# Graph layer on one core: the node table in groups of four blocks, loads and stores reordered

## What is computed

```python
h = relu(layernorm(x))                        # per node
l0 = h[:, :64] @ W_l1_0 * a / sqrt(64)        # node table, a = node_vec1
l1 = einsum('nud,uw->nwd', h[:, 64:], W_l1_1) * a / sqrt(32)
w  = relu(edge_attr_10 @ W_fc1 ...) @ W_fc2   # 192 weights per edge
y0, y1 = l0[src], l1[src]                     # gather per edge
m  = products of w, y0, y1 and edge_attr_4    # messages
s  = segment_sum(m, dst)                      # per node
out = x + self-interaction(h) + s @ W_l2
```

## Time and profile before

| | us |
|---|---|
| median of 3 runs | 4271.78 (4270.87 to 4272.3) |
| the profiled execution | 4272.76 |
| its span in the profile | 4268.9 |
| PE busy (share of the span) | 3722.5 (87%) |
| POOL busy | 3100.0 (73%) |
| DVE busy | 2009.8 (47%) |
| ACT busy | 1025.5 (24%) |
| mean granted clock of PE | 0.791 |

### The profile page before, as it was taken

The page is one execution under the profiler, slowest core; times in us unless marked ns, Lnnn a source line. Parts: engine busy times, 40 slices in busy tenths (PEclk is TensorE's granted clock), DMA queues, the critical chain, the costliest instruction groups (busy, mean ns, idle before and its releaser), DMA issues.

```text
span 4268.9 us, 57575 instructions
## 1 busy us (share of the span) xinstructions
PE 3722.5 (87%) x17362; PEld 2092.9 (49%) x17362; DVE 2009.8 (47%) x6987; ACT 1025.5 (24%) x2226; POOL 3100.0 (73%) x3265
## 2 busy tenths in 40 slices
PE   7988888888888888889888888888888888888887
PEld 6644444444444444444444544554444454444444
DVE  5345444444544444444444444444444444444443
ACT  3322222222222222222222222222222222222222
POOL 1277777777777777777777777777777777777775
PEclk9978777787777878777877877777788787877877
DMA  5245455555555454555545455554545555455454
GB/s 173 68 125 140 130 136 131 137 132 132 136 134 138 129 137 131 135 131 137 139 130 138 128 138 135 133 138 129 137 131 137 137 131 138 130 136 139 129 138 109
DMA packets 717859, 566.78 MB, mean 133 GB/s; under 512 B 394563, under 2 KB 646098, under 8 KB 717168
## 3 DMA queue, kind: packets, MB, share of 16 engines
q0 software_dynamic: 155008, 265.22, 26.1%
q1 hardware_dynamic: 562064, 297.63, 24.4%
q10 hardware_dynamic: 480, 0.19, 0.0%
HBM read 414.55 MB, written 148.11 MB: 132 GB/s over the span
## 4 chain that ended last, share of the span: by engine, by line
POOL 35%; DMA 25%; PE 17%; issue 14%; DVE 9%; SPq 0%; ACT 0%; ACTq 0%; DVEq 0%; POOLq 0%
POOL R L588 35%; DMA R<-l_table,src 24%; DVE R L696 6%; PE bank L734 5%; PE bank L461 3%; DVE R L693 3%; PE bank L724 2%; PE bank L747 2%; PE bank L304 1%; PE bank L302 1%; PE bank L291 1%; PE bank L503 0%; PE bank L292 0%; DMA av<-in_avec 0%; PE bank L484 0%
## 5 line engine op out<-in xcount | busy, mean ns | idle before, releaser
L588 POOL DMA_INDIRECT R<-l_table,src x3223 | 3070.1, 953 | 1003.3 <-issue 799.6
L734 PE MATMUL bank<-w,hs 100*128 100x192 f32 x6446 | 1685.4, 404 | 510.0 <-DVE R L696 504.0
L734 PEld LDWEIGHTS bank<-w,hs 100*128 100x128 f32 x6446 | 1302.7, 233 | 1124.2 <-issue 1062.0
L693 DVE TENSOR_TENSOR R<-bank,R 128x256 f32<-128x256 f32 x1612 | 682.1, 423 | 2057.1 <-DMA R<-l_table,src 1115.5
L696 DVE TENSOR_TENSOR R<-bank,R 128x192 f32<-128x192 f32 x3224 | 984.6, 347 | 0.0
L654 ACT ACTIVATE E<-bank 128x320 f32<-128x320 f32 x806 | 352.3, 437 | 2390.2 <-PE bank L747 2345.1
L747 PE MATMUL bank<-R 128*32 128x320 f32 x6448 | 758.7, 550 | 0.0
L724 PE MATMUL bank<-ea,w1s 10*100 10x512 f32 x1612 | 569.5, 789 | 0.8 <-ACT hs L648 0.8
L648 ACT ACTIVATE hs<-bank 100x512 f32<-100x512 f32 x806 | 436.7, 594 | 391.3 <-PE bank L724 390.7
L461 PE MATMUL bank<-Z,D 128*128 128x448 f32 x784 | 419.5, 690 | 6.3 <-DMA Z<-s_tiles 6.3
L461 PEld LDWEIGHTS bank<-Z,D 128*128 128x128 f32 x784 | 184.1, 248 | 267.6 <-issue 260.0
(11 more groups left out here) (69 smaller groups left out, 771.7 us busy)
## 6 DMA issues: line engine op xcount, KB each, us to landing
s_tiles<-E SPq DMA_DIRECT2D x806, 160.0 KB
R<-l_table,src POOLq DMA_INDIRECT x3223
ea<-in_ea_p SPq DMA_DIRECT2D x403, 96.0 KB
Z<-s_tiles SPq DMA_DIRECT2D x392, 96.0 KB
Z<-s_tiles SPq DMA_DIRECT2D x392, 80.0 KB
Z<-s_tiles SPq DMA_DIRECT2D x392, 48.0 KB
x<-in_xp SPq DMA_DIRECT2D x14, 560.0 KB, 7.1
l_table<-ls SPq DMA_DIRECT2D x14, 560.0 KB, 3.1
```

Source lines behind the costliest of these rows:

```text
L588: PL.indirect_dma_start(out=Y[:, g % NB, t, :], out_offset=None, in_=T, in_offset=bass.IndirectOffsetOnAxis(ap=src[:, k:k + 1], axis=0),). ...
L693: V.tensor_tensor(p[:, :, :, 0:64], w[:, :, 0:128].rearrange("p t (s c) -> p t s c", s=2), y[:, :, 0:64].unsqueeze(2).to_broadcast([128, n ...
L734: m = PE.matmul(b[:, o * 192:(o + 1) * 192], hs[:, g % 4, t * 128:(t + 1) * 128], w2[:, :], start=True, stop=True, skip_group_check=True)
```

## The change

It regroups the table stage by four blocks, 640 columns, which are five times 128:

- `centre` writes into one buffer `H` (2 x 640 columns), whichever engine it is on.
- `turn(q)` transposes five full 128x128 parts of four blocks; a part can hold the end of one block and the beginning of the next.
- `lin(q)` multiplies by five pieces of a block-diagonal 640x640 matrix, laid out on the host as `bl` (128x704): three of 128 columns, two of 160 that overlap in 32 columns, where the two halves of a block are added in PSUM.
- `keep_wide` (DVE, 512 columns at once) and `keep_fifth` (ACT) copy the transposed parts; `row_out` reads five pieces for four blocks (block 2 lies in two banks).
- `ls` holds 3 x 4 blocks, and SP stores every four, 25 stores instead of 14.
- SP's queue has all of x first; the scaling of the weights on DVE moves behind the first statistics; ACT runs one square root ahead of everything; the end of the window test and the flag move to the end of the stage.

Core of the diff:

```diff
-        hn = sb("hn", [128, 3, C])
-        hp = sb("hp", [128, 2, C])
-        hta = sb("hta", [128, 2, 256])
-        htb = sb("htb", [32, 2, 256])
-        ls = sb("ls", [128, 2, LC, C])
+        H = sb("H", [128, 2, 4 * C])
+        hta = sb("hta", [128, 2, 512])
+        htb = sb("htb", [128, 2, 128])
+        ls = sb("ls", [128, 3, 4, C])
...
         for c in range(NLC):
             SP.dma_start(x[:, c * LC:(c + 1) * LC, :], xv[:, c * LC:(c + 1) * LC, :]).then_inc(s_x[c], 16)
-            if c == 1:
-                SP.dma_start(bas[:, :, :], a["bases"].rearrange("o (g t) -> o g t", t=G).to_broadcast([128, NG, G])
-                             ).then_inc(s_b, 16)
...
+        SP.dma_start(bound[:, :, :], a["bound"]).then_inc(s_b, 16)
...
         def row_out(j):
-            c, jj = divmod(j, LC)
+            q, b = divmod(j, 4)
             if j % BC == 0:
                 AC.wait_ge(s_ar, j // BC + 1)
...
+            if b == 0 and q >= 3:
+                AC.wait_ge(s_T[q % 3], 16 * (q // 3))
+            fore, rear = bank[4 + q % 2], bank[6 + q % 2]
...
+        def turn(q):
+
+            if q >= 2:
+                PE.wait_ge(s_ha, q - 1)
+                PE.wait_ge(s_hb, q - 1)
+            for j in blocks(q):
+                if j % 3 == 2:
+                    PE.wait_ge(s_hp, third.index(j) + 1)
+                else:
+                    PE.wait_ge(s_hn, others.index(j) + 1)
+                b = j % 4
+                m = PE.transpose(bank[q % 2][:, b * 128:(b + 1) * 128], H[:, q % 2, b * 128:(b + 1) * 128], ident[:, :])
...
+            PE.transpose(bank[2 + q % 2][:, 0:128], H[:, q % 2, 512:640], ident[:, :]).then_inc(s_tp, 1)
+
+        def lin(q):
+            fore, rear = bank[4 + q % 2], bank[6 + q % 2]
+            PE.wait_ge(s_ha, q + 1)
+            if q >= 2:
+                PE.wait_ge(s_lv, rows_out(q - 2))
+            for b in range(3):
+                k = slice(b * 128, b * 128 + 128)
+                m = PE.matmul(fore[:, k], hta[:, q % 2, k], bl[:, k], start=True, stop=True, skip_group_check=True)
+            m.then_inc(s_lp, 1)
+            PE.matmul(rear[:, 0:160], hta[:, q % 2, 384:512], bl[:, 384:544], start=True, stop=False,
                       skip_group_check=True)
+            PE.wait_ge(s_hb, q + 1)
+            PE.matmul(rear[:, 96:256], htb[:, q % 2, :], bl[:, 544:704], start=False, stop=True,
                       skip_group_check=True).then_inc(s_lp, 1)
...
+        for q in range(NQ + 2):
+            if q >= 2:
+                for j in blocks(q - 2):
+                    row_out(j)
+            if 1 <= q <= NQ:
+                keep_fifth(q - 1)
+            if q + 1 < NQ:
+                for j in blocks(q + 1):
+                    centre(j)
+            if q in batch:
+                root(batch[q])
...
         stats(0)
+        map_weights()
         stats(1)
         deviations(0)
-        nst, ndv = 2, 1
+        nst = 2
         pieces = test()
-        for i in range(NT // 2):
+        for q in range(NQ):
+            while nst < NLC and nst * LC < 4 * q + 16:
                 stats(nst)
                 nst += 1
+            keep_wide(q)
+            if q in batch:
+                deviations(batch[q])
+            if q == min(10, NQ - 1):
                 main_weights()
+            if q >= 8:
                 next(pieces, None)
...
-        for c in range(NLC):
-            SP.wait_ge(s_lv, (c + 1) * LC)
-            SP.dma_start(tv[:, c * LC:(c + 1) * LC, :], ls[:, c % 2, :, :]).then_inc(s_T[c % 2], 16)
+        for q in range(NQ):
+            n = len(blocks(q))
+            SP.wait_ge(s_lv, rows_out(q))
+            SP.dma_start(tv[:, 4 * q:4 * q + n, :], ls[:, q % 3, 0:n, :]).then_inc(s_T[q % 3], 16)
```

More of the change, by code:

```diff
@@ L151, in build @@
         s_ha = sem("s_ha")
-        s_hb = [sem("s_hb0"), sem("s_hb1")]
+        s_hb = sem("s_hb")
         s_lp = sem("s_lp")
         s_lv = sem("s_lv")
-        s_T = [sem("s_T0"), sem("s_T1")]
+        s_T = [sem(f"s_T{b}") for b in range(3)]
         s_one = sem("s_one")
@@ L295, in lin @@
[L295 to L302, removed]
+            if b == 0 and q >= 3:
+                AC.wait_ge(s_T[q % 3], 16 * (q // 3))
+            fore, rear = bank[4 + q % 2], bank[6 + q % 2]
+            if b == 0:
+                AC.wait_ge(s_lp, 2 * q + 1)
@@ L303, in lin @@
                       skip_group_check=True)
-            PE.matmul(ov[:, 128:160], htb[:, i % 2, o * 128:o * 128 + 128], blb[:, :], start=False, stop=True,
+            PE.wait_ge(s_hb, q + 1)
+            PE.matmul(rear[:, 96:256], htb[:, q % 2, :], bl[:, 544:704], start=False, stop=True,
                       skip_group_check=True).then_inc(s_lp, 1)
-        FP = max(NT // 2 - 7, 1)
         PE.wait_ge(s_w, NW)
-        PE.wait_ge(s_pw, 1)
-        for j in range(NT + 3):
-            if j < NT:
-                turn(j)
-            if j >= 3:
-                lin(j - 3)
-            if j == 2 * FP + 4:
+        for q in range(NQ + 1):
+            if q < NQ:
+                turn(q)
+            else:
@@ L317, in build @@
                 PE.wait_ge(s_fl, 1)
                 PE.wait_ge(s_one, 1)
-                PE.matmul(bank[2][32:33, 0:1], vio[:, 8:9], ones[:, :], start=True, stop=True,
+                PE.matmul(bank[q % 2][0:1, 0:1], vio[:, 8:9], ones[:, :], start=True, stop=True,
                           skip_group_check=True).then_inc(s_fl, 1)
-        LAG = 6
-        AC.wait_ge(s_w, NW)
-        root(0)
-        for j in range(NT + LAG):
-            if j < NT and j % BC == BC - 3 and j + 3 < NT:
-                root(j // BC + 1)
-            if j < NT:
-                centre(j)
-            if j >= 3 and j % 2 and (j - 3) // 2 < NT // 2:
-                narrow((j - 3) // 2)
-            if j >= LAG:
-                row_out(j - LAG)
-            if j == 2 * FP + 5:
+            if q == 1:
+                PE.wait_ge(s_pw, 1)
@@ new lines, in build @@
+            if q:
+                lin(q - 1)
+        batch = {-(-c * BC // 4): c for c in range(1, NBC)}
+        AC.wait_ge(s_one, 1)
+        AC.activation(warm[:, :], ones[:, :], ACT.Sqrt)
+        for j in blocks(0):
+            centre(j)
+        root(0)
+        for q in range(NQ + 2):
+            if q >= 2:
+                for j in blocks(q - 2):
[4 more added lines that the diff above has]
+                for j in blocks(q + 1):
+                    centre(j)
+            if q in batch:
+                root(batch[q])
+            if q == NQ:
@@ L335, in build @@
                 AC.wait_ge(s_fl, 2)
-                AC.activation(flag[0:1, 0:1], bank[2][32:33, 0:1], ACT.Copy).then_inc(s_fs, 1)
+                AC.activation(flag[0:1, 0:1], bank[q % 2][0:1, 0:1], ACT.Copy).then_inc(s_fs, 1)
         def test():
@@ L549, in table_there @@
         def table_there():
-            PL.wait_ge(s_T[0], 16 * ((NLC + 1) // 2))
-            PL.wait_ge(s_T[1], 16 * (NLC // 2))
+            for b in range(3):
+                PL.wait_ge(s_T[b], 16 * ((NQ + 2 - b) // 3))
         with nc.If(way == 0):
@@ L916, in lay_out @@
     ea_p[:, 32:42] = both[:, 1]
-    bla = np.zeros((128, 128), f)
-    bla[0:64, 0:64] = v["L0_gnn_W_l1_0"]
-    bla[64:96, 64:96] = v["L0_gnn_W_l1_1"]
-    bla[96:128, 96:128] = v["L0_gnn_W_l1_1"]
+    one = np.zeros((C, C), f)
+    one[0:64, 0:64] = v["L0_gnn_W_l1_0"]
+    for d in range(3):
+        one[64 + 32 * d:96 + 32 * d, 64 + 32 * d:96 + 32 * d] = v["L0_gnn_W_l1_1"]
+    four = np.zeros((4 * C, 4 * C), f)
+    for b in range(4):
+        four[b * C:(b + 1) * C, b * C:(b + 1) * C] = one
+    bl = np.concatenate([four[128 * b:128 * b + 128, o:e] for b, (o, e) in
+                         enumerate(((0, 128), (128, 256), (256, 384), (384, 544), (480, 640)))], axis=1)
     pw = np.zeros((5 * 128, C), f)
```

101 lines of the change are left out of this document (52 added, 49 removed).

## The result

| | kernel before | changed kernel |
|---|---|---|
| median of 4 runs (us) | 4271.61 (4270.87 to 4272.3) | 4196.35 (4193.85 to 4196.62) |
| span of the profiled execution (us) | 4268.9 | 4192.6 |
| first gather starts (us) | 185.3 | 108.3 |
| last gather starts (us) | 4236.6 | 4161.8 |

The changed kernel is faster by 75.3 us, a ratio of 0.9823 (95% interval 0.9806 to 0.984). The forecast was 4204.5 with a range of 4190 to 4214. The first gather was forecast at 118.0 and came 9.7 earlier.

The account below looks back on a forecast made before the run. POOL's gathers bound the kernel, PE the table stage before them. 43.0 + 5.2 + 62.1 + 2.5 + 1.1 + 0.2 = 114.1 put the first gather at 118.0, saving 67.3 us: 4204.5, range 4190 to 4214.

Parts of the forecast that it names:

- rival 1: Table stage: PE's clock rises, DVE and ACT pace at 2.9 to 3.0 us per four, 4194.5 us; chance 0.24.
- What bounds: Main stage: POOL's gathers pace it; only what the table stage saves before the first gather comes off the whole.
- PE's four at 1.2 GHz: Table stage: PE takes 3.45 us per four blocks, bounds 3.4 and 4.15, as nearly nothing changes shape.
- The stall: Table stage: ACT stops some 15 us until the first table store, queued behind the loads, lands at 43.0 (38 to 45).
- Rival 2: First table store not held behind the loads: no stall, first gather near 106, 4192.5 us; chance 0.08.
- I keep 1.2 GHz: Table stage: PE's clock stays at 1.2 GHz under the new instruction mix, as in the old stage.
- the charge for DVE: Table stage: 1.1 us (0 to 6) where main-weight scaling falls beside a window-test piece and statistics.
- Level with PE: Table stage: DVE's work per four sums to 3.5 us, about PE's 3.45.
- The other engines: Table stage, per four: ACT 2.4 us and POOL 1.1, both hidden below PE's 3.45.
- Rival 3: Table stage: PE still pays for shapes, or DVE paces; 3.85 us per four, 4212.5 us; chance 0.13.
- rival 4: Main stage passes from POOL to PE at mean clock 0.65: slower, 4394 us; chance 0.02.
- The start gains: Start of table stage: early x and the root's table load ahead of time are worth nothing, hidden by the stall.

Follow-up runs that it names:

- all three cures: Changed kernel with six-four row buffer, later stages' loads behind table stores, main-weight scaling on POOL instead of DVE: 4156.28 us against 4273.37 for the kernel before.
- kernel with 128 rows: Kernel before with second transpose 128 columns wide and second product over 128 rows, 96 against zeros: ratio 0.9866, repeated 0.9871.
- x first: Kernel before with only SP's loads reordered, all of x first in the queue, run twice: ratios 0.9998 and 1.0003.
- wide transpose: Kernel before with second transpose 128 columns wide, second product on rows 96 to 127 alone: 5260.32 us against 5265.68, ratio 0.9992.

## Why the prediction was right, and where it was not

**The number.** 4196.35 lies in the stated range of 4190 to 4214, but 8.2 us under the forecast's own 4204.5. It is in the range because the range took in rival 1, and rival 1 is what happened: its 4194.5 stands on a first gather at about 108, and that came at 108.3. The forecast's own path (PE at 1.2 GHz from end to end) did not hold.

**What bounds: right.** 77.0 us at the first gather, 75.3 in the time; what else the traces show in the main stage is no more than its variants scatter by. That *nothing* outside the main stage can touch it was too strong in general: with all three cures it lost 23 us.

**PE's four at 1.2 GHz: right.** 3.45 forecast, 3.41 measured. The reason given, that time is lost by going between shapes, was right in kind. The experiments name the shape: the 32-row product, at 0.44 us a block (1.61 to 1.17). The narrow transpose, which changes shape too, costs nothing (1.60 with the wide one).

**The stall: right.** Forecast some 15 us, up to 43.0; measured 15.14, up to 43.65. Rival 2 is out.

**The step that failed: "I keep 1.2 GHz".** The clock rose, which was rival 1. That rival said DVE and ACT would then pace at 2.9 to 3.0 per four and the time be 4194.5; measured were 3.05 and 4196.35. The closeness is in part luck: the rival has PE at 2.4 GHz throughout, while in about 20 of the 55 us it was back at 1.2. The argument against it, 155 us of unbroken work at 1.2 GHz, was a true reading of the old kernel but no evidence for the new one, since the cause was the 32-row product that the change removes. The kernel with 128 rows rises, the one with rows 96 to 127 alone doesn't, in two kernels that are otherwise alike.

The Trainium skill, "TensorE: Matmul & The Clock Gate", in its table "Why this matters for your kernels", has a busy TensorE get the full clock. The changed stage agrees (full speed from 23.5 us); the stages with 32-row products, busy 10.00 of 10 us at 1.2 GHz, do not. The same page's "Part 4: PE-mode transpose", that transposes don't count as PE-busy in the same way, stood beside the failed step as fitting it. The rise came in a mix with 5 transposes in 15 instructions, so that rule did not hold it back here.

Term by term, from 118.0 to 108.3. The last lin's products on the timeline of PE give two of the times:

```profile
104.26 0.94 PE L323 MATMUL bank<-bl,hta 128*128 128x128 f32 x6
105.03 0.44 PE L325 MATMUL bank<-bl,hta 128*128 128x160 f32 x2
105.30 0.49 PE L328 MATMUL bank<-bl,htb 128*128 128x160 f32 x2
```

| term | forecast | measured | difference |
|---|---|---|---|
| store 0 lands | 43.0 | 43.65 | +0.6 |
| to the end of lin(5), 49.37 | 5.2 | 5.7 | +0.5 |
| 18 fours, and the charge for DVE | 62.1 + 1.1 | 104.26 - 49.37 = 54.9 | -8.3 |
| last lin, 104.26 to 105.79 | 2.5 | 1.5 | -1.0 |
| last copies, store, POOL's start | 4.1 | 2.5 | -1.6 |

A four is 54.9 / 18 = 3.05 us where 3.45 was forecast. It isn't 1.76, since DVE now sets most of the pace, and behind PE's waits the clock is low again (71.51 to 74.75 and 94.99 to 98.41 are fours of 3.24 and 3.42). "Level with PE" was right at the old clock, and it made DVE's sum the one that counted at the new one. The store was mis-sized at 3.1, which is the time of the old 560 KB; the last one holds two blocks, 160 KB, and took 1.94. There is also a slip in the forecast's 5.2: its own terms (1.3 + 0.3 + 0.9, 0.5, 2.4) make 5.4.

**The other engines: nearly as forecast.** ACT and POOL stay hidden but for the stall and two waits of PE for ACT's copy (1.03 us up to 66.05, 1.16 up to 89.28); ACT's 9.66 of 10 us from 50 to 60 is the catching up behind it. **Rival 3** (3.85 per four) and **rival 4** (the main stage passes to PE) did not happen: PE's main work is 3567.8 us at 0.78.

**The start gains: right as to the changed kernel.** They were booked at nothing because the stall hides them. The loads in the old order cost 1.5 us at the first gather, within what runs of one kernel differ by.

## What to carry to other kernels

When one pair of instructions in a busy TensorE loop costs more than its size explains, pad it to full rows against zeros before counting instructions: here that alone brought 68 to 72 of the 77 us. Work out the next engine's sum per step whenever a clock could double, as that sum is then what counts. And a store issued behind big loads in one queue can land late (15 us here against 2.4); order the queue by who needs what first, or give the ring enough slots to outlast it.

## What the runs showed of the hardware

- A float32 product over 32 rows among products over 128 slowed its neighbour too: the full pair ahead of it takes 0.56 to 0.57 us instead of 0.43, itself 0.56 instead of 0.28, at 1.2 GHz.
- With such products in the loop, PE stayed at 1.2 GHz while busy for 10.00 of 10 us, for 140 to 150 us, in three kernels (before, x first, wide transpose). Without them it rose in every kernel, within 10 us of the first product. This is shown for this mix alone: the main stage has products over 10 rows (L724 in the kernel before, `10*100` on its page) among others, and its mean granted clock is 0.78.
- PEclk reads 1.00 at both speeds: the earlier trace rows with transposes 0.21 to 0.27 apart, and the changed kernel from 100 to 110 us with 0.11. In the first stage of these profiles the spacing of equal instructions tells the clock, the column doesn't.
- An indirect gather of the same shape took 946, 949 and 946 ns (medians) in the three runs of one kernel and 953 to 957 in its relatives. Between the last run and the kernel before that was 23 us of the main stage; the cause is open.
